# First attention of a two-layer decoder: normed rows copied by GpSimd, and the place of the next low half

## The reference, cut to what matters

```python
def _layernorm(x, axis=-1, eps=1e-05):
    m = jnp.mean(x, axis=axis, keepdims=True)
    v = jnp.var(x, axis=axis, keepdims=True)
    return (x - m) / jnp.sqrt(v + eps)
...
    q = (x @ Wq).reshape(b, n, H, DH)      # H = 16 heads of 64; k and v alike
    scores = jnp.einsum('bihd,bjhd->bhij', q, k) * scale + bias[None]   # causal, ALiBi
    attn = jax.nn.softmax(scores, axis=-1)
    out = jnp.einsum('bhij,bjhd->bihd', attn, v).reshape(b, n, H * DH)
    return out @ Wo + bo
...
x = x + _L0_attn_ref(_layernorm(x, axis=-1), ...)
x = x + _L0_xattn_ref(_layernorm(x, axis=-1), ctx_1024, ...)
```

## Time and profile before

| what | value |
|---|---|
| median of 3 runs | 1607.67 us (1607.4 to 1609.68) |
| the profiled execution | 1606.57 us, its span 1604.8 us |
| PE busy | 1454.2 us, 91% of the span |
| PEld busy | 1104.2 us, 69% |
| DVE busy | 1086.4 us, 68% |
| ACT busy | 1021.9 us, 64% |
| POOL busy | 500.5 us, 31% |

### The profile page before, as it was taken

How to read it: one execution, slowest core, us unless ns; L and a number is a source line. 1 busy time by engine, 2 the same in 40 slices (tenths; PEclk the granted TensorE clock), 3 DMA queues, 4 the chain that set the end, 5 groups by cost and what they waited for, 6 DMA issues and landing times. The chain is left out here.

```text
span 1604.8 us, 39544 instructions
## 1 busy us (share of the span) xinstructions
PE 1454.2 (91%) x11655; PEld 1104.2 (69%) x11703; DVE 1086.4 (68%) x3495; ACT 1021.9 (64%) x2734; POOL 500.5 (31%) x845
## 2 busy tenths in 40 slices
PE   7999999999999877779999969988999886999998
PEld 5777777777777644558888846655665555777697
DVE  6776777777777557656666636787778764774665
ACT  7887777777777536366666646666666663653454
POOL 4332333332333226123333222322323204541133
PEclk9999999999999988779999988999999998998999
DMA  6000000000000041001111110000000000000000
GB/s 214 2 0 0 0 0 0 0 0 0 0 0 0 2 164 33 14 16 44 43 43 45 38 55 14 14 7 13 13 13 11 8 1 1 2 1 1 1 27 26
DMA packets 34077, 34.76 MB, mean 22 GB/s; under 512 B 5600, under 2 KB 29792, under 8 KB 33248
## 3 DMA queue, kind: packets, MB, share of 16 engines
q1 hardware_dynamic: 29664, 25.07, 4.8%
q0 software_dynamic: 4352, 8.92, 2.2%
HBM read 25.07 MB, written 8.91 MB: 21 GB/s over the span
## 5 line engine op out<-in xcount | busy, mean ns | idle before, releaser
L622 POOL TENSOR_SCALAR a_prob<-a_prob,a_inv 128x128 f32<-128x128 f32 (+1 forms) x256 | 126.4, 504 | 346.8 <-DVE a_inv L511 346.8
L441 ACT ACTIVATE a_prob<-a_psS,a_low 128x128 f32<-128x128 f32 (+1 forms) x512 | 208.8, 427 | 1.1 <-DVE a_low L501 1.1
L501 DVE CUSTOM_DVE_ANT_0 a_psS<-a_psS,a_bias 128x128 f32<-128x128 f32 (+1 forms) x512 | 167.4, 388 | 37.7 <-PE a_psS L315 18.3
L1805 ACT ACTIVATE a_probT<-a_psZ 128x512 f32<-128x512 f32 x256 | 138.8, 594 | 75.2 <-PE a_psZ L1591 75.2
L1888 DVE TENSOR_REDUCE a_low<-a_psS 128x4 f32<-128x1024 f32 x128 | 156.2, 1220 | 27.0 <-PE a_psS L1591 25.9
L432 ACT COPY a_probT<-a_psT 128x384 f32<-128x384 f32 x256 | 123.2, 481 | 74.3 <-PE a_psT L361 66.1
L361 PE MATMUL a_psT<-ident,a_prob 128*128 128x128 f32 x768 | 132.7, 282 | 4.5 <-ACT a_probT L432 2.4
L1332 POOL DMA_INDIRECT d_rows<-rows_dram,source x72 | 67.9, 943 | 191.2 <-PE e_psX L1414 143.3
L315 PE MATMUL a_psS<-a_qk 64*128 64x128 f32 (+1 forms) x1024 | 119.9, 353 | 1.1 <-ACT a_qk L424 1.0
L361 PEld LDWEIGHTS a_psT<-ident,a_prob 128*128 128x128 f32 x768 | 84.7, 140 | 45.6 <-issue 34.8
L351 PE MATMUL a_psO<-a_probT,a_v 128*64 128x256 f32 (+1 forms) x1024 | 111.5, 339 | 0.6 <-DVE a_o L525 0.6
(11 more groups left out here) (375 smaller groups left out, 4160.0 us busy)
## 6 DMA issues: line engine op xcount, KB each, us to landing
sorted_out<-e_y SPq DMA_DIRECT2D x72, 64.0 KB, 1.6
in_lo<-in_gate_up SPq DMA_DIRECT2D x4, 1024.0 KB, 6.9
x<-in_x SPq DMA_DIRECT2D x8, 256.0 KB, 6.1
down<-in_down SPq DMA_DIRECT2D x1, 2048.0 KB, 15.1
rows_dram<-rows SPq DMA_DIRECT2D x8, 256.0 KB, 2.2
out<-x SPq DMA_DIRECT2D x8, 256.0 KB, 2.3
d_rows<-rows_dram,source POOLq DMA_INDIRECT x72, 2.7
a_sel_in<-in_sel SPq DMA_DIRECT2D x1, 1024.0 KB, 4.9
```

What stands on the lines that cost most here:

```text
L441: nc.scalar.activation(prob[:, 2 * (p % 4) + k, lo:hi], psS[:, u, lo:hi], ACT.Exp, bias=low[:, u, i:i + 1], scale=-1.0, accum_out=total[:, ...
L501: nc.vector.tensor_tensor_reduce(psS[:, u, lo:hi], psS[:, u, lo:hi], bias0[:, 2 * p + k, lo:hi], 1.0, LEAST, ALU.add, ALU.min, low[:, u, i ...
L622: nc.gpsimd.tensor_scalar(w, w, inv[:, 2 * (q % 2) + 1, i:i + 1], 1.0, ALU.mult, ALU.mult).then_inc(norm_done[1], 1)
L1805: nc.scalar.activation(probT[:, (p + half + 1) % 2, 2 * half + c, :, :].rearrange("p j s -> p (j s)"), psZ[:, c, :], ACT.Exp, scale=-1.0). ...
```

## The change

`apply` writes each block once, to the scratch tile. `g.rows` is now written by POOL: `add_rows`, in slot 6, first copies both blocks (128x256) from the scratch tile with one `tensor_copy`, waits for it, and then does its addition. Since the scratch tile is read by POOL too, `apply` waits for the copy of the batch before (`rows_kept`). Apart from this, `split_next(b + 1)` goes from the end of slot 6 to its beginning, ahead of `lows(b, 6)` in DVE's list.

```diff
--- before.py
+++ after.py
@@ -127,12 +127,17 @@
         dve.wait_ge(self.rstd_done, b + 1)
         if not (isinstance(b, int) and b < ahead):
             dve.wait_ge(self.turned, START + b - ahead + 1)
+            if self.keep_rows:
+                dve.wait_ge(self.rows_kept, START + b)
         for k in range(BT):
-            args = (self.source[:, bass.ds(b * BT + k, 1), :], self.moments[:, j, k, 0:1], self.power[:, j, k:k + 1],
-                    ALU.subtract, ALU.mult)
-            nc.vector.tensor_scalar(self.rows[:, j, k, :], *args).then_inc(self.rows_done, 1)
-            if self.keep_rows:
-                nc.vector.tensor_scalar(g.rows[:, bass.ds(b * BT + k, 1), :], *args).then_inc(self.rows_kept, 1)
+            nc.vector.tensor_scalar(self.rows[:, j, k, :], self.source[:, bass.ds(b * BT + k, 1), :], self.moments[:, j, k, 0:1],
+                                    self.power[:, j, k:k + 1], ALU.subtract, ALU.mult).then_inc(self.rows_done, 1)
+
+    def copy_rows(self, pool, b, seen, j=0):
+
+        pool.wait_ge(self.rows_done, b * BT + BT)
+        pool.sem_inc(seen, 1)
+        self.nc.gpsimd.tensor_copy(self.g.rows[:, bass.ds(b * BT, BT), :], self.rows[:, j, :, :]).then_inc(self.rows_kept, 1)
 
     def turn(self, pe, b, out, j=0):
 
@@ -536,6 +541,8 @@
                         ln.stats_landed(dve, b - 1)
                         dve.sem_inc(seen, 1)
                         ln.aggregate(dve, b - 1)
+                    if prep and p == 6:
+                        split_next(b + 1)
                     if new:
                         lows(b, p, has_unit)
                     if has_unit(p, 1):
@@ -552,8 +559,6 @@
                         nc.vector.tensor_tensor(g.x[:, bass.ds((b - 1) * BT, BT), :], resid[:], g.bo[:], ALU.add).then_inc(x_done, 1)
                     if has_unit(p, 3):
                         keep_o(b, p)
-                    if prep and p == 6:
-                        split_next(b + 1)
                     if prep and p == 1:
                         ln_in.stats(dve, b + 1)
                     if prep and p == 2:
@@ -593,6 +598,7 @@
 
         @block.gpsimd
         def _(pool):
+            pool.sem_inc(ln.rows_kept, START)
             nc.gpsimd.memset(g.eps[:], LN_EPS).then_inc(const_set, 1)
             nc.gpsimd.memset(g.minus_half[:], -0.5).then_inc(const_set, 1)
             pool.wait_ge(const_set, 2)
@@ -636,7 +642,8 @@
 
             def add_rows(b):
                 at = bass.ds(b * BT, BT)
-                pool.wait_ge(ln.rows_kept, b * BT + BT)
+                ln.copy_rows(pool, b, pool_seen)
+                pool.wait_ge(ln.rows_kept, START + b + 1)
                 pool.sem_inc(pool_seen, 1)
                 nc.gpsimd.tensor_tensor(g.x[:, at, :], g.x[:, at, :], g.rows[:, at, :], ALU.add)
```

## The result

The changed kernel takes 1602.34 us (median of 20 runs, 1598.1 to 1606.67) against 1607.54 us (20 runs, 1603.97 to 1611.72): a ratio of 0.9969, interval [0.996, 0.9977], 5.2 us less where 10.2 were forecast. The profiled execution took 1603.42 us, its span 1601.7 us.

What follows compares the result with a forecast made beforehand. PE bounds the first attention, waiting for VectorE in slot 7. 14 rounds x 0.70 = 9.8 us plus 0.4 in the last round give 10.2, so 1607.67 becomes 1597.5 us; range 1594.5 to 1602.5.

Steps and rivals of the forecast that it cites:

- Where PE waits, and how much can be had: Slot 7, first attention: PE's projection waits for `next_lo`, last in VectorE's full queue, which takes 0.77 us of each round.
- What is late next: End of slot 7: PE's transposition of normed rows waits for VectorE's copy of values, leaving 0.70 us gained a round.
- part 2: Slot 6: the difference made first costs VectorE 0.33 us wherever it stands; `lows` start at 237.19 instead of 237.32.
- part 1: VectorE's queue: two of four row writes leave, 0.26 us each, making it 0.52 us shorter.
- signs that the prediction named for being wrong: VectorE idle over 0.1 us before the difference, scaling later than 0.86 us behind slot 7's scores, or waiting during POOL's copy.
- The signal from VectorE to PE: End of slot 7: PE goes on 0.05 us after VectorE's copy of values ends, at 242.12.
- The distance from L146 to the next scores: End of slot 7: the last 0.45 us, from transposition of normed rows to next scores, taken as unchanged.
- bound for signals: Loop rounds: signals and queueing three times dearer cost 0.2 us more a round, leaving 7.4 us gain, 1600.3 us.
- The copy on POOL: POOL, slot 6: copy 0.45 us, wait for its end 0.1, additions 0.73 everywhere; costed at nothing for PE.
- Rival 2: POOL's copy blocks VectorE for its whole 0.45 us; a round gains 0.25 us, time 1603.8 us; chance 0.07.
- The rival on the slower side: Slot 6: the difference waits for ScalarE, delaying `lows` by x; at x = 1.47 us, 12.6 us slower, 1619.9; chance 0.04.
- Rival 1: Another wait, ScalarE's copy of the transposed tile or POOL's `norm`, replaces the removed one in full; 1607.3 us; chance 0.05.

Runs made afterwards that it cites:

- e3: Changed kernel with VectorE's copy of values ahead of `invert` in slot 7; ratio to the kernel before 0.993, slot 7 3.94 us.
- e10: Changed kernel with values ahead of `invert`, difference behind `lows`, ScalarE's rounding later in slot 6, POOL's power ahead of `norm` in slot 5; 1589.1 us, ratio to before 0.9895.
- e2: Kernel before with only `split_next` moved to the beginning of slot 6, rows still written twice by VectorE; ratio to before 0.9995.
- e5: Changed kernel with the low half (the difference) made directly behind `lows` of slot 6, not ahead; ratio to the kernel before 0.9949.
- e4: Changed kernel with one more VectorE copy of 128x256 ahead of the copy of values in slot 7; ratio to the kernel before 1.0001.
- e1: Kernel before with only the copy on POOL, the low half still made at the end of slot 6; ratio to before 0.998.
- e9: Kernel before with POOL making the layer norm's power ahead of its `norm` in slot 5; ratio to before 0.9962.

## Why the prediction was right or wrong

- **Where PE waits, and how much can be had** (0.77 us a round, only slot 7, only through VectorE): right. All other slots last what they did, the wait for `next_lo` is gone, and e3 and e10 realise the whole 0.77 and a little more.
- **What is late next**: right in name. PE waits for the copy of values at the end of slot 7. VectorE's chain to it was 4.45 us (4.46). The 0.42 us of the round of b = 15 came as well (0.43), and b = 0 lost nothing in slot 7 (0.86 us from scores to transposition).
- **The step that failed is part 2**, "the difference costs 0.33 us wherever it stands", started at 0.57 us behind the first row write. It began at 0.73. The prediction allowed 0.05 us between ScalarE's end and VectorE's start; the trace shows 0.24. A full queue hides what lies between a wait that is met and the instruction behind it (e2 and e5: the difference costs 0.34 us, nothing is idle); a queue that stands in the wait does not. With it `lows` came 0.04 us later than before instead of 0.13 sooner, and the 0.52 us of part 1 were used up at once. Mis-sized by 0.17 us; e5 took 0.22 out by moving the difference behind `lows`. Two of the signs that the prediction named for being wrong came true here: VectorE idle ahead of the difference, and the transposition of slot 7 later than 0.86 us behind its scores (0.91).
- **The signal from VectorE to PE**: 0.05 us allowed, 0.15 measured (241.13 to 241.28). Mis-sized by 0.10 us, although the trace of before had the price: PE's projection started at 240.43, 0.14 us behind the end of the difference at 240.29.
- **The distance from L146 to the next scores** was kept at 0.45 us without a word. It became 0.59, the way back over the loop's edge paid behind a wait (e4): 0.14 us, missing in the sum. Together 0.17 + 0.10 + 0.14 = 0.41; 0.70 - 0.41 = 0.29 us, the measured gain. 14 x 0.29 = 4.1 us; the loop as a whole gave 3.96, where 9.8 was forecast. The last round gave its 0.4 us as forecast, and the 0.17 us by which the first round ended later is scatter. The prediction's bound for signals (0.2 us more a round) was half of what three small errors of one sign made.
- **The copy on POOL**: 0.39 us for 0.45, hidden, additions 0.73 us as forecast; the wait between the two took 0.26 us and not 0.1, hidden too. Rival 2 was dismissed on one row ("there it was POOL that paid"). That row held for one order of starts. The copy does not hold VectorE in the changed kernel because the difference was moved away from it, which the prediction did not count as the move's merit: e1 shows the price without it, 0.24 us a round. By the rule that the prediction names first (the Trainium skill, SBUF — State Buffer, Who interferes with whom), an instruction of VectorE with two inputs in SBUF and a GpSimd instruction that reads SBUF exclude each other, and the one that starts first wins. e1 and e9 agree in who waits; how much the loser waits is less than its whole length, as it ends 0.28 us behind the winner and takes 0.41 alone. The other rule named there, on the 2-port modes, no run here tests.
- **The rival on the slower side** (VectorE waits for ScalarE in slot 6) was the right mechanism at small size: x was 0.04 and not 1.47 us. Rival 1 did not occur in full, but over half of the wait removed came back in other places.
- **The range** held the median (1602.34 us) only just, at its upper end of 1602.5, and the chance for a clear gain was right, but the forecast gain was twice the measured one.

## What to carry to other kernels

Count a shortened queue as won only up to the next wait in it: an instruction moved to a place where its input is just ready costs its latency of waking too, and one place later in the list may cost nothing. Before work goes to GpSimd, list what VectorE runs beside it, and keep its readers away from VectorE's instructions with two inputs in SBUF; the start, not the length, decides who pays. And look where the late queue begins before trimming it: here the order of two helpers on GpSimd, for which VectorE waited 0.92 us at the head of the queue, was worth more than the two writes.

## What the runs showed of the hardware that I had not expected

- The difference on VectorE (two SBUF inputs, 128x256 fp32) took 0.41 to 0.43 us alone, 0.65 us when a GpSimd copy of 0.39 us had begun 0.02 us ahead of it, and 0.90 us when an addition of 0.72 us had begun 0.10 us ahead. Both times it ended 0.28 us behind GpSimd's end. When both began within 0.01 us of each other (before), GpSimd's addition took 1.01 instead of 0.73 us and the difference 0.41.
- Inside the hardware loop an engine that stands in a wait started 0.24 us (VectorE behind ScalarE) and 0.14 to 0.15 us (PE behind VectorE) behind the end of its releaser. Where the same code is written out with constants it was about 0.1 less: 0.15 us at the kernel's start (8.02 to 8.17, changed kernel) and 0.14 in slot 6 of b = 0 (35.23 to 35.37), 0.05 us in the round of b = 15 (546.37 to 546.42, before; 0.05 to 0.06 in each of the nine traces in which PE waits there). In the loop alone the trace has register work at that place (L581, DVEq, 65 ns). That this makes the whole difference fits, but no run took it away. Behind GpSimd's power VectorE started after 0.04 us in the loop (235.15 to 235.19), so it is no fixed price of a wait; spans on POOL are rough.
- PE's distance across the loop's edge is 0.37 us with a full queue (e3), 0.42 to 0.45 before, 0.58 to 0.59 behind a wait from b = 4 on, and does not grow with that wait (e4). Where PE leaves the loop it is 0.36 to 0.37 in every trace, with a wait and without, and the branch at the edge takes 83 ns there against 215 (changed kernel, L188).
